# Set-up of a graph layer: edge arrays and mixing weights loaded before the accumulators' clears, turns regrouped, clears of 33 KB rows

## The reference

```
xn  = layernorm(x)
agg = segment_sum(edge_weight[:, None] * (xn @ W_l)[src], dst, N)
x   = x + (agg + b_l + xn @ W_r + b_r) + mix(xn)      # linear attention, gate, projection
x   = x + moe(layernorm(x))                           # 8 experts, 2 for each node
```

## Time and profile before

| | us |
|---|---|
| median of 3 runs (lowest, highest) | 4630.21 (4624.43, 4647.81) |
| the profiled execution's own time | 4624.93 |
| its span | 4623.2 |
| POOL busy | 3185.6 |
| PE busy | 3404.9 |
| DVE busy | 2512.0 |
| ACT busy | 1694.8 |
| moved in DRAM, written | 401.47 MB |

### The profile page before, as it was taken

One profiled execution on the slowest core, in us unless ns is written; L12 is line 12 of the kernel. 1 busy time (PEld: TensorE's weight loads), 2 busy tenths in 40 slices (PEclk: granted clock), 3 DMA queues, 4 the chain that ended last, 5 costly groups with the idle time before them and its releaser, 6 DMA issues. The chain is left out here.

```text
span 4623.2 us, 85711 instructions
## 1 busy us (share of the span) xinstructions
PE 3404.9 (74%) x16479; PEld 2839.6 (61%) x16636; DVE 2512.0 (54%) x11283; ACT 1694.8 (37%) x3127; POOL 3185.6 (69%) x2213
## 2 busy tenths in 40 slices
PE   0266666667666667887888788887388839999999
PEld 0255555555555556666666666666277728888888
DVE  0577777766555556666666666665278822222222
ACT  0033333334444433444444444444122214443443
POOL 0088888888888888888888888888545624444555
PEclk9788788888888888888888888888699969999999
DMA  9388888877777777777777777777799856665555
GB/s 400 120 149 146 152 151 152 150 113 109 113 116 115 115 101 104 107 107 106 107 106 102 106 107 106 107 107 98 136 316 290 264 132 144 145 142 156 175 176 152
DMA packets 603960, 670.63 MB, mean 145 GB/s; under 512 B 62751, under 2 KB 556797, under 8 KB 599281
## 3 DMA queue, kind: packets, MB, share of 16 engines
q0 software_dynamic: 275904, 286.40, 47.1%
q1 hardware_dynamic: 269232, 283.76, 20.9%
q10 hardware_dynamic: 58752, 99.69, 6.0%
HBM read 270.03 MB, written 401.47 MB: 145 GB/s over the span
## 5 line engine op out<-in xcount | busy, mean ns | idle before, releaser
L750 POOL DMA_INDIRECT agg<-msg,sidx x1664 | 2580.2, 1551 | 727.5 <-issue 408.5
L1078 PE MATMUL bank<-rows,Cmat 128*128 x3328 | 1019.4, 447 | 165.8 <-ACT msg L1271 139.0
L1271 ACT COPY msg<-bank 128x512 f32<-128x512 f32 x832 | 487.2, 586 | 1476.2 <-DMA agg<-msg,sidx 1195.5
L1078 PEld LDWEIGHTS bank<-rows,Cmat 128*128 128x128 f32 x3328 | 694.0, 223 | 343.6 <-issue 251.0
L818 DVE SCALAR_TENSOR_TENSOR sidx<-seen_sum,trash,srcf 128x4 int32<-128x4 f32 x416 | 92.7, 223 | 1025.9 <-DMA agg<-msg,sidx 1023.2
L1062 PE MATMUL bank<-Emat,pick 128*128 128x128 f32 x3328 | 528.4, 311 | 131.4 <-DVE seen L805 115.5
L801 DVE TENSOR_SCALAR Emat<-bank,srcf,wtf 128x128 f32<-128x128 f32 x1664 | 565.4, 401 | 0.0
L1062 PEld LDWEIGHTS bank<-Emat,pick 128*128 128x128 f32 x3328 | 516.9, 226 | 40.0 <-issue 16.2
L805 DVE SCALAR_TENSOR_TENSOR seen<-bank,srcf,prior 128x128 f32<-128x128 f32 x1664 | 480.8, 345 | 0.0
L1982 PE MATMUL bank<-x_xf,x_w 128*128 128x256 f32 x1792 | 407.3, 380 | 1.3 <-ACT x_xf L2010 1.3
L1992 PE MATMUL bank<-ffn_w,x_hT 128*128 x1792 | 407.0, 380 | 0.0
(11 more groups left out here) (249 smaller groups left out, 4396.9 us busy)
## 6 DMA issues: line engine op xcount, KB each, us to landing
x_w<-in_L_ffn_W_dram SPq DMA_DIRECT2D x112, 512.0 KB, 4.2
agg<-zeros ACTq DMA_DIRECT2D x36, 1408.0 KB, 36.3
r_agg<-agg SPq DMA_DIRECT2D x196, 256.0 KB, 5.0
x_zin<-expert_table SPq DMA_DIRECT2D x112, 259.0 KB, 4.5
window_raw<-in_x_dram SPq DMA_DIRECT2D x208, 128.0 KB
agg<-msg,sidx POOLq DMA_INDIRECT x1664
xn_rows<-n_xn ACTq DMA_DIRECT2D x49, 256.0 KB, 4.1
xn_turned<-n_xnT ACTq DMA_DIRECT2D x49, 256.0 KB, 4.6
```

The costliest lines, as they stand in the source:

```text
L750: pool.indirect_dma_start(scratch["agg"][r][:, :], bass.IndirectOffsetOnAxis(ap=sidx[:, j:j + 1], axis=0), msg[:, j % (2 * BATCH), :], Non ...
L1078: mm = nc.tensor.matmul(M[p][:, (q % 2) * D:(q % 2 + 1) * D], Cmat[:, b % 2, q, :], rows[:, bass.ds(slot, 1), :], start=True, stop=True)
L1271: nc.scalar.copy(msg[:, at:at + 2, :].rearrange("p q c -> p (q c)"), M[p][:, :]).then_inc(s_msg, 1)
```

## The change

The edge arrays are loaded on two queues, each array with its own semaphore: SP has `dst` (and `raw_end`) and behind it the 14 arrays of mixing weights, which come from `edge_phase`; ACT has `src`, the edge weights and `wide`. The clears stand on ACT's queue behind these, `zeros` holds 33 rows to a partition, and 12 DMAs do it: 7 right away, 5 after ACT's copies. PE turns `flt_loc` first, then `src`, weights and `dst`, 13 tiles each, four tiles to a bank; DVE copies `flt_loc` out, ACT the other three and also casts `src` and `packed`. The preparation of the mixing weights moves into `setup_phase`. `dst` is kept as float (`dstf`).

```diff
-CLEAR_ROWS = 11
+CLEAR_ROWS = 33
...
         @block.sync
         def _(sp):
-            sp.wait_ge(s_clear, 6)
...
+            sp.wait_ge(s_clear, 2)
+            load_edges(sp, raw["dst"], t["dst"], s_dst)
             sp.dma_start(raw_end[0:rest_rows, :],
...
+            for to, a in weights:
+                sp.dma_start(to, a, allow_slow_non_contiguous=True).then_inc(s_w, 16)
 
             sp.wait_ge(s_win, WPLAN)
...
         @block.scalar
         def _(act):
 
+            act.wait_ge(s_clear, 5)
+            load_edges(act, raw["src"], t["src"], s_src)
+            load_edges(act, raw["wt"], t["edge_weight"], s_wt)
...
             act.wait_ge(s_clear, 6)
-            for n in range(CLEARS):
-                for acc in scratch["agg"]:
-                    act.dma_start(acc[n * CLEAR_ROWS * P:(n + 1) * CLEAR_ROWS * P, :].rearrange("(p a) d -> p (a d)", p=P),
-                                  zeros[:]).then_inc(s_zeroed, 16)
+            for acc, n in clears[:READY]:
+                act.dma_start(clear_rows(acc, n), zeros[:]).then_inc(s_zeroed, 16)
+
+            act.wait_ge(s_src, 48)
+            nc.scalar.copy(flt["src"][:], raw["src"][:]).then_inc(s_fsrc, 1)
+            n = 0
+            for to in (srcf, wtf, dstf):
+                for four in FOURS:
+                    act.wait_ge(s_turn, n + 1)
+                    nc.scalar.copy(to[:, four[0] * P:(four[-1] + 1) * P], psum[n % 4][:, 0:len(four) * P]).then_inc(s_taken, 1)
+                    n += 1
+            act.wait_ge(s_masked, 2)
+            nc.scalar.copy(edges["packed"][:], wide[:])
+            for acc, n in clears[READY:]:
+                act.dma_start(clear_rows(acc, n), zeros[:]).then_inc(s_zeroed, 16)
+            act.wait_ge(s_pprep, 2)
+            nc.scalar.copy(mix["hbias"][:], psum[4][:, 0:GH])
+            nc.scalar.copy(mix["wqT"][:].rearrange("p a n -> p (a n)"), psum[5][:, :])
...
         @block.vector
         def _(dve):
...
-            dve.wait_ge(s_load, 16 * 11)
-            nc.vector.tensor_copy(flt["src"][:], raw["src"][:]).then_inc(s_flt, 1)
+            dve.wait_ge(s_dst, 16 * 5)
             nc.vector.tensor_copy(flt["dst"][:], raw["dst"][:]).then_inc(s_flt, 1)
...
             assert done[0] == WPLAN
+            dve.wait_ge(s_wide, 96)
+            nc.vector.tensor_scalar(wide[0:SPAN], wide[0:SPAN], (P - 1) * P, None, ALU.bitwise_and).then_inc(s_masked, 1)
+            nc.vector.tensor_scalar(wide[SPAN:P], wide[SPAN:P], P - 1, None, ALU.bitwise_and).then_inc(s_masked, 1)
             dve.wait_ge(s_wturn, 5)
...
             assert done[0] == WLOCAL
...
+            dve.wait_ge(s_w, WEIGHTS)
...
+            for n, four in enumerate(FOURS):
+                dve.wait_ge(s_loc, n + 1)
+                nc.vector.tensor_copy(locf[:, four[0] * P:(four[-1] + 1) * P], psum[6 + n % 2][:, 0:len(four) * P]).then_inc(s_ltaken, 1)
```

More of the change, by code:

```diff
@@ new lines, in setup_phase, with load_edges @@
+        WEIGHTS = 16 * len(weights)
+        clears = [(acc, n) for acc in scratch["agg"] for n in range(CLEARS)]
+        READY = 7
+        def load_edges(engine, to, a, done):
+            engine.dma_start(to[:, 0:full_tiles, :],
+                             a[0:full_tiles * P * P].rearrange("(t c p) -> c t p", c=P, p=P)).then_inc(done, 16)
+            engine.dma_start(to[0:rest_rows, full_tiles, :],
+                             a[full_tiles * P * P:EFULL * P].rearrange("(c p) -> c p", p=P)).then_inc(done, 16)
+            engine.dma_start(to[rest_rows:rest_rows + 1, full_tiles, 0:rest],
+                             a[EFULL * P:E].rearrange("(a p) -> a p", a=1)).then_inc(done, 16)
@@ L281, in _ @@
             assert done[0] == WLOCAL
[L283 to L294, removed]
+            dve.wait_ge(s_w, WEIGHTS)
+            nc.vector.tensor_tensor(mix["bsum"][:], mix["brows"][:, 0, :], mix["brows"][:, 1, :], ALU.add).then_inc(s_prep, 1)
+            for a in range(HALF):
+                nc.vector.tensor_scalar(mix["wg1s"][:, a, :], mix["wg1"][:, a, :], mix["lng"][:, a:a + 1], None, ALU.mult)
+                nc.vector.tensor_scalar(mix["lnb_all"][:, a, :], ones[:], mix["lnb"][:, a:a + 1], None, ALU.mult)
+            nc.vector.tensor_scalar(mix["bg2h"][:], mix["bg2"][:], 0.5, None, ALU.mult).then_inc(s_prep, 1)
+            dve.wait_ge(s_prep, 1)
+            nc.vector.tensor_tensor(mix["bsum"][:], mix["bsum"][:], mix["brows"][:, 2, :], ALU.add)
+            for n, four in enumerate(FOURS):
+                dve.wait_ge(s_loc, n + 1)
+                nc.vector.tensor_copy(locf[:, four[0] * P:(four[-1] + 1) * P], psum[6 + n % 2][:, 0:len(four) * P]).then_inc(s_ltaken, 1)
+            nc.vector.tensor_tensor(edges["both"][:], ident[:, 0:SPAN], ident[:, SPAN:P], ALU.add)
         @block.gpsimd
@@ L337, in _, with edge_phase @@
             pe.wait_ge(s_win, WLOCAL)
[L338 to L344, removed]
+            for n, four in enumerate(FOURS):
+                if n >= 2:
+                    pe.wait_ge(s_ltaken, n - 1)
+                for i in four:
+                    mm = nc.tensor.transpose(psum[6 + n % 2][:, (i - four[0]) * P:(i - four[0] + 1) * P],
+                                             flt["loc"][:, i, :], ident[:])
+                mm.then_inc(s_loc, 1)
+            pe.wait_ge(s_fsrc, 1)
+            turn(flt["src"], FOURS)
+            pe.wait_ge(s_wt, 48)
+            turn(raw["wt"], FOURS)
+            turn(flt["dst"], FOURS)
+            pe.wait_ge(s_w, WEIGHTS)
+            pe.wait_ge(s_prep, 2)
+            for a in range(HALF):
+                nc.tensor.matmul(psum[4][:, 0:GH], mix["lnb_all"][:, a, :], mix["wg1"][:, a, :], start=(a == 0), stop=False)
+            nc.tensor.matmul(psum[4][:, 0:GH], ones[0:1, :], mix["bg1"][:], start=False, stop=True).then_inc(s_pprep, 1)
+            for a in range(HALF):
+                for b in range(HALF):
+                    last = nc.tensor.transpose(psum[5][:, a * D + b * P:a * D + (b + 1) * P],
+                                               mix["wq"][:, b, a * P:(a + 1) * P], ident[:])
+            last.then_inc(s_pprep, 1)
 def first(i):
     return isinstance(i, int) and i == 0
-def edge_phase(nc, t, scratch, psum, ident, prior, trash, ones, gscale, edges, s_zeroed):
+def edge_phase(nc, t, scratch, psum, ident, prior, trash, ones, gscale, edges, mix, s_zeroed):
     with ExitStack() as ctx:
@@ L655, in _ @@
             load_window(0, 1)
-            for dst, src in weights:
-                sp.dma_start(dst, src, allow_slow_non_contiguous=True).then_inc(s_w, 16)
             load_x(0, 0)
@@ L772, in _ @@
             dve.wait_ge(s_blank, 2)
[L773 to L786 removed]
+            nc.vector.tensor_copy(gidx[:], dstf[:, 0:CHUNK_GROUP]).then_inc(s_gidx, 2)
             def picks(g, b):
```

175 lines of the change are left out of this document (80 added, 95 removed).

## The result

| | before | changed |
|---|---|---|
| median of the runs, us | 4632.36 (4624.43 to 4647.81, 4 runs) | 4557.76 (4556.57 to 4562.81, 4 runs) |
| ratio, 95% interval | | 0.9837 (0.981 to 0.9864) |
| profiled execution: time, span | 4624.93, 4623.2 | 4562.81, 4560.9 |
| first add, last add on POOL | 222.1, 3313.2 | 159.0, 3248.0 |

The changed kernel is faster by 1.6%. From profile to profile the span is 62.3 us shorter. The first add comes 63.1 us earlier, the last one 65.2 us, and what follows the last add is 3 us longer. So the whole gain is made ahead of the first add, and nearly all of it arrives.

What follows compares the result with a forecast made beforehand. POOL's adds run at a fixed pace after the first add, which waits for clears and message. First add -62 us and quicker first adds -2 gave 4624.9 - 64 = 4561 profiled, forecast 4563 us, range 4545 to 4588.

Steps and rivals of the forecast that it cites:

- What bounds the kernel: POOL: 1664 adds at one per 1.85 us follow the first add, so its shift reaches the end one for one.
- (a): Set-up loads put ahead of the clears: 34 us on the most loaded DMA engine (29 to 41), 25 if evenly spread.
- (b): Clears after the loads: 51.9 MB at 425 GB/s, 122 us, all cleared at 159 us (146 to 166).
- (c): Chain from `dst` through set-up, windows and x to the first message: ready at 149, ten us before the clears.
- (d): The sum: first add at 160 instead of 222.1, -62 us, and -2 from quicker first adds.
- the -2: POOL's first adds: messages made ahead save most of their slower start, 2 us.
- 1 (message late): Rival: the message, not the clears, sets the first add, near 169 or 195; 4570 to 4600 us; chance 0.15.
- its second form: Weights still queued when clears start wait 1.27 us a packet: first add near 195, 4598 us; within rival 1's 0.15.
- 2: Rival: clears or loads faster than taken, first add about 140; 4538 to 4550 us; chance 0.12.
- 3: Rival: 33 KB runs clear slowly, kernel slower than before; at 220 GB/s about 4675 us; chance 0.03.
- 4: Rival: adds slow down or a later block waits for something else, under 23 us gained; chance 0.03.
- ACT's hold till 68: Profile sign: ACT held at the second batch of clears, its queue full, till near 68 us.

Runs made afterwards that it cites:

- spread: Changed kernel with loads of 124 rows cut into 112 and 12 and of 31 into 16 and 15: first add 150.3, ratio to before 0.9817.
- spread_two_queues: spread with the second half of `wide` loaded on SP's queue ahead of the weights: first add 172.4, ratio to before 0.9884.
- after_third: The changed kernel repeated unchanged on a later chip: first add 158.7, median 4586.41 us, ratio to before 0.9863.
- before_loads_first: Kernel before, with its 36 clears of 11 KB rows held until the edge loads have landed: first add 182.9, ratio 0.9917.
- mix_in_edge: Changed kernel with the mixing weights' loads and preparation put back into the second block: first add 175.6, ratio to before 0.9831.
- after_again: The changed kernel repeated unchanged on a later chip: first add 159.1, median 4575.49 us, ratio to before 0.9846.
- spread_late_wait: spread with POOL's wait for the clears moved to right before its first add: first add 150.2, ratio to before 0.9848.

## Why the prediction was right

- **What bounds the kernel** (the first add, then 1664 adds at POOL's pace): right. Over all versions the first add lay between 150 and 229, and the last add went with it: the distance was between 3087.6 and 3092.6 in all of them. That is 1.859 us an add and not 1.85, so the last add before is at 3313 and not 3300; it is the same in both kernels and cancels.
- **(a) Small loads, 34 us on the most loaded engine, 29 to 41.** Right in mechanism and nearly in size. `wide` was in use at 36.12 where I had 38. `dst` was there by 11.5 where I had 16: the two queues' small packets overlapped (DMA share 1.15, 287 GB/s in 5:10), but with 2450 packets in these 5 us it was 33 ns for each on an engine, hardly under my 35, so most of these 4.5 us stays open. The four and one engines were the case that I took against an even spread; `spread` shows the even spread to be 9.5 us quicker, as the 9 us between my 34 and 25.
- **(b) Clears 122 us at 425 GB/s, ended at 159 (146 to 166).** 426 GB/s in 40:60, no gap behind the seventh, last packets in 156:157. Right in rate and mechanism. What I had not seen is that only the loaded engines end so late; the others were through at 149. They did not start when their loads were out, but when ACT issued the clears, at 26.41.
- **(c) The message.** DVE's chain from `flt_dst` to `cfit` took 9.0 us as forecast (11.51 to 20.54). `bsum` came at 48 where I had 50, the cast took 3.26 us for my 3.3, the turns and copies 10 for my 11 (48.0 to 58.2). The weights were in time, as I had taken. The set-up was over near 64 and not 70: ACT was held at its queue for 1.6 us only, until 62.9 and not 68. In `spread` it was held 6.7 us, until 58.1, with the clears at full rate from 25: 33 us, three clears and a bit, so about nine fit the queue, near the ten that I had taken. It is the earlier start of the clears on most engines (26.4 and not 37) that made the hold short; that is worked out, not tested. Windows and x: 52 packets from 67.6 to 131.7 are 1.23 us each for my 1.27. Message at 140.6 where I had 149: 5.4 us from the earlier window load (67.6 for 73), 1.8 from the packets, 1.2 from the statistics to the message. Its cover is 18 us, not 10.
- **(d) The sum.** First add at 158.95 for 160; -63.1 for -62. That it is so close is in part luck: the last packets of the clears came in 156:157 and not at 159, and from there to the first add it was some 2.5 us where my sum has 1. The first adds did come quicker, the fifth 7.6 us after the first instead of 10.3, but the -2 does not show in the whole: from first to last add it is 3089.1 us here and 3091.1 before, but 3090.7 and 3088.1 in the two repeats. Profile to profile -62.3 for -64. The median 4557.76 lies 5 us under my 4563, since I had allowed part of the 5 us by which the profiled execution of before lay under its median, and the changed kernel's own lay above it.
- **Rivals.** 1 (message late) did not happen here, though spread_two_queues shows that its second form is real: first add 172.4, where I had 195 for all weights behind the clears. 2 did not either, though its small loads were a little quicker than taken, see (a); the clears moved at 426 GB/s now and at 425 with 11 KB packets. The gain of 8% for DMAs of 4.3 MB that I had worked out as an estimate from the Trainium skill, page "DMA: Bandwidth & Descriptors", section "Bandwidth", is not borne out by that. 3 falls with the same number. 4: the gain arrived.
- **What would show it**: POOL released by the clears, no wait of DVE for the weights, one add per 1.85 us, all so. Of the signs that I forecast, ACT's hold till 68 is the one that hardly showed, and the releaser reads "issue" in this profile and the clears only in after_third.

Three things that I did not have in the prediction are in the experiments: that ACT's full queue holds the end of the block (93 us in before_loads_first), which the prediction used for `hbias` alone; that this, and no DMA rate, is why the long clears help; and that the weights, put ahead, delay ACT's clears by 9.4 us (26.41 against 16.97 in mix_in_edge).

## What to carry to other kernels

Find the two things that the first instruction of the pacing engine waits for, and treat each as a budget: here the bulk clears at the DMA engines' full rate, and the chain to the first message; what is small goes wholly ahead of the bulk, on both queues evenly, for a small packet left behind it costs a full turn of a big packet. Do the parts together: loads first gave 39 of the 63 us, long clears alone made it 7 us worse, and the weights had to come out of the stream as well. Set the small tiles before the large one when a queue waits for them: the longer memset in front of the first load was 5.9 of those 7 us. Cut loads whose row count is no multiple of 16, and read the end of a stream by DMA share: a share of 0.33 at its tail was 9 us.

## What the runs showed of the hardware that I had not expected

- Between a queue of 33 KB packets and one of 512 B packets the engines took one from each in turn (1555 and 1553 packets in 110 us), with no regard to size.
- Two queues of small packets side by side gave a DMA share of 1.15 and 287 GB/s (5:10 of the changed kernel), where one queue with 1 KB packets gave 356 and one with the rows of `wide` 197.
- An engine that issues DMAs is held while its queue is full, 93 us for 36 clears, and with it the end of its block.
- The kernel's total varies by up to 63 us between runs on the later chips (4553.17 to 4616.64 in after_third), with the first add equal within 0.4 us. In the waits of 3230:4700, of the changed kernel first and then of after_again:

```profile
PE bank L1991 <- DMA x_zin<-expert_table: 79.3, 7, 70.5
```

```profile
PE bank L1991 <- DMA x_zin<-expert_table: 117.3, 47, 68.8
```

PE waits 38 us more for the experts' table, in 47 waits instead of 7, of 48.7 us between the spans (4560.9 and 4609.6). `spread` has 118.2 us in 49 waits at a span of 4600.3, `spread_late_wait` 75.5 in 3 at 4545.9. It comes with versions of either kind; what makes it stays open.
